# Rounding eight one-hot tables between other copies, and loading them in two pieces, in a recommendation tower

## The reference

```
e = stack([tbl_t[ids[:, t]] for t in range(26)])          # 2048 x 26 x 128
combined = concatenate([dense[:, None, :], e], axis=1)    # 27 features
interactions = einsum('bfd,bgd->bfg', combined, combined)[:, iu, ju]   # upper triangle
h = concatenate([dense, interactions, dense], axis=1)
h = maximum(h @ W_top1 + b_top1, 0)                       # 607 -> 512
h = maximum(h @ W_top2 + b_top2, 0)                       # 512 -> 256
y = h @ W_top3                                            # 256 -> 1
```

## Time and profile before

| | |
|---|---|
| median of three executions | 431.84 us |
| the profiled execution | 434.48 us, of which the span is 432.7 us |
| PE busy | 369.9 us (86%) |
| POOL busy | 276.1 us (64%) |
| DVE busy | 256.5 us (59%) |
| ACT busy | 114.2 us (26%) |
| mean granted clock of TensorE | 0.942 of full |

### The profile page before, as it was taken

The page is one execution under the profiler, slowest core; times in us unless marked ns, Lnnn a source line. Parts: engine busy times, 40 slices in busy tenths (PEclk is TensorE's granted clock), DMA queues, the critical chain, the costliest instruction groups (busy, mean ns, idle before and its releaser), DMA issues.

```text
span 432.7 us, 6765 instructions
## 1 busy us (share of the span) xinstructions
PE 369.9 (86%) x2792; PEld 332.1 (77%) x2792; DVE 256.5 (59%) x368; ACT 114.2 (26%) x235; POOL 276.1 (64%) x295
## 2 busy tenths in 40 slices
PE   0560499996499959999999999999999999999797
PEld 0450499996499948997799979986999799678663
DVE  3254199998088833875389838952588566106410
ACT  2110333322122331322232333322123412321210
POOL 6772277777777777777777777777777777710000
PEclk9996599999599969999999999999899999989999
DMA  5659535444244433444343424343433332310000
GB/s 129 178 165 231 183 84 117 87 79 101 52 93 79 98 56 54 87 100 106 55 91 79 103 52 92 78 100 79 93 77 77 56 53 53 78 21 0 2 0 1
DMA packets 50941, 35.89 MB, mean 83 GB/s; under 512 B 6136, under 2 KB 44664, under 8 KB 50912
## 3 DMA queue, kind: packets, MB, share of 16 engines
q0 software_dynamic: 41472, 18.89, 24.7%
q1 hardware_dynamic: 9440, 16.58, 13.0%
HBM read 35.44 MB, written 0.01 MB: 82 GB/s over the span
## 4 chain that ended last, share of the span: by engine, by line
PE 58%; POOL 18%; issue 7%; DMA 6%; SPq 5%; DVE 3%; ACT 2%; DVEq 0%
POOL E L239 18%; PE psG L347 17%; PE psB L322 16%; PE psB L391 8%; PE psB L398 6%; DMA ET<-tbl 6%; PE psB L386 4%; PE psB L307 3%; SPq L254 2%; PE psB L358 2%; PE psB L405 2%; SPq L251 1%; SPq L247 1%; DVE S L574 1%; PE psB L372 1%
## 5 line engine op out<-in xcount | busy, mean ns | idle before, releaser
L239 POOL DMA_INDIRECT E<-tbl,gidx x288 | 275.4, 956 | 103.9 <-issue 87.0
L552 DVE TENSOR_TENSOR one_hot<-oidx,psR 125x1024 fp32r<-125x1024 int32 x128 | 152.3, 1215 | 39.0 <-PE psB L322 32.2
L322 PE MATMUL psB<-one_hot,tab_hi 125*128 125x256 f32 x512 | 143.2, 311 | 19.5 <-DVE tab_lo L557 13.4
L322 PE MATMUL psB<-one_hot,tab_lo 125*128 125x256 f32 x512 | 133.4, 292 | 0.0
L322 PEld LDWEIGHTS psB<-one_hot,tab_hi 125*128 125x128 f32 x512 | 103.0, 201 | 21.7 <-issue 13.8
L347 PE MATMUL psG<-ET 128*108 128x108 f32 x1024 | 112.5, 265 | 2.0 <-ACT ET L486 1.0
L347 PEld LDWEIGHTS psG<-ET 128*108 128x108 f32 x1024 | 106.6, 180 | 3.1 <-DVE S L574 1.6
L574 DVE COPY_PREDICATED S<-own,psG 108x216 f32<-108x216 int32 x192 | 77.1, 402 | 51.1 <-ACT S L508 44.5
L322 PEld LDWEIGHTS psB<-one_hot,tab_lo 125*128 125x128 f32 x512 | 103.1, 201 | 0.6 <-issue 0.5
L307 PE MATMUL psB<-ident_r,E 128*128 128x128 f32 x288 | 36.7, 253 | 32.0 <-ACT ET L501 18.3
L307 PEld LDWEIGHTS psB<-ident_r,E 128*128 128x128 f32 x288 | 31.0, 145 | 36.4 <-issue 20.0
(11 more groups left out here) (34 smaller groups left out, 149.7 us busy)
## 6 DMA issues: line engine op xcount, KB each, us to landing
oidx<-hot_idx SPq DMA_DIRECT2D x32, 256.0 KB, 3.5
E<-tbl,gidx POOLq DMA_INDIRECT x288
ET<-tbl SPq DMA_DIRECT2D x8, 500.0 KB
dense<-dense_pairs SPq DMA_DIRECT2D x8, 128.0 KB, 3.6
Zd<-dense_rows SPq DMA_DIRECT2D x4, 256.0 KB, 3.1
UH<-W_pairs SPq DMA_DIRECT2D x1, 768.0 KB, 18.6
S<-W_dense SPq DMA_DIRECT2D x1, 512.0 KB, 21.1
w<-W SPq DMA_DIRECT2D x1, 512.0 KB, 13.4
```

The source lines that it names most:

```text
L239: nc.gpsimd.indirect_dma_start(E[:, n % SLOTS, i, :], None, gathered[2 * (n % T_GROUPS) + i // 2].bitcast(f32r), bass.IndirectOffsetOnAxis ...
L322: product = nc.tensor.matmul(bank[:, t % 2 * DUO:(t % 2 + 1) * DUO], tab[0:ROWS_P, t, r, :], one_hot[0:ROWS_P, m % RING, kc, :], start=(r ...
L552: nc.vector.tensor_tensor(one_hot[0:ROWS_P, m % RING], ids, rows, ALU.is_equal).then_inc(hot_full[m % RING], 1)
```

## The change

The change has three parts.

1. ScalarE rounds tables 0 and 1 ahead of the list, and tables 2 to 7 one by one at every second chunk of period 0, where VectorE has its splits already.
2. Each table is loaded by two DMAs, one of 112 partitions (`SPREAD_P`) and one of 13, on the same semaphore; ScalarE waits for 32 instead of 16.
3. SyncE's order: fill 1 and the first dense part come behind table 2, fill 2 behind table 5; the second part of the gather indices and the second dense part come behind table 7.

```
+    SPREAD_P = ROWS_P // 16 * 16
...
             def load_table(h):
-                sp.dma_start(raw_table(h), small[h].rearrange("(p k) d -> p (k d)", k=ROWS_K)
-                             ).then_inc(table_in[h], 16)
+                rows = small[h].rearrange("(p k) d -> p (k d)", k=ROWS_K)
+                for part in (slice(0, SPREAD_P), slice(SPREAD_P, ROWS_P)):
+                    sp.dma_start(raw_table(h)[part], rows[part]).then_inc(table_in[h], 16)
...
             load_oidx(0)
-            load_table(0)
-            load_table(1)
-            sp.dma_start(gidx[:, first:], gather_idx[:, first:]).then_inc(gidx_in[1], 16)
-            for h in range(2, RAW):
+            for h in range(RAW):
                 load_table(h)
-                if h == 3:
+                if h == 2:
                     load_oidx(1)
-                    load_oidx(2)
-            load_dense(0)
-            load_dense(1)
+                    load_dense(0)
+            load_oidx(2)
             for h in range(RAW, NS):
                 sp.wait_ge(lo_ready, h - RAW + 1)
                 load_table(h)
+            sp.dma_start(gidx[:, first:], gather_idx[:, first:]).then_inc(gidx_in[1], 16)
+            load_dense(1)
...
-                act.wait_ge(table_in[h], 16)
+                act.wait_ge(table_in[h], 32)
...
-            for h in range(NS):
+            for h in range(2):
                 round_table(h)
+            rounded_tables = 2
...
-                    elif step[0] == "hot" and step[2] % FILL_CHUNKS == FILL_CHUNKS - 1:
-                        empty_hot(step[1], step[2])
+                    elif step[0] == "hot":
+                        if d == 0 and step[2] % 2 == 0 and rounded_tables < NS:
+                            round_table(rounded_tables)
+                            rounded_tables += 1
+                        if step[2] % FILL_CHUNKS == FILL_CHUNKS - 1:
+                            empty_hot(step[1], step[2])
```

## The result

| | before | changed |
|---|---|---|
| median of 4 executions | 432.36 us (431.76 to 433.13) | 419.44 us (418.33 to 422.52) |
| the profiled execution | 434.48 us, span 432.7 | 420.29 us, span 418.3 |

The ratio is 0.971, 95% interval 0.965 to 0.977: 12.9 us faster in the medians, 14.2 in the profiled executions. Forecast were 417.8 us, 14.0 us faster, and a range of 413.0 to 422.5.

The account below looks back on a forecast made before the run. GpSimd's gather stream was taken as the floor up to turn 71, with a 50.1 us TensorE tail. -14.6 + 0.6 = -14.0 us; 431.84 - 14.0 = 417.8 us, the forecast's own range 414 to 421.5, stated range 413.0 to 422.5.

Parts of the forecast that it names:

- GpSimd's stream is the floor: GpSimd's gathers bound the run up to turn 71; what counts is their earlier end, not TensorE's 18.3 us stall.
- Rival D: TensorE is the bound and its stall and waits all go, 32 us: 399.8 us; chance under 0.01.
- 14.63 us off the stream: GpSimd's 14.93 us stall before gather 24 goes entirely, less the normal 0.30 us.
- +0.6 us for the eighth split: VectorE's eighth table split, formerly inside GpSimd's stall, now has a gather beside it and lengthens it: +0.6 us.
- Faster landing, 2.5 to 3 us a table: Two DMAs per table on SyncE's queue land a table in 2.5 to 3 us instead of 5.49.
- The deadline of 68.0: TensorE's first gram must start by 68.0 us to reach turn 17 when gather 71's data is there; forecast 60.
- Part 1 is what takes the stall away: ScalarE's new rounding order alone removes GpSimd's whole stall; earlier tables are worth nothing directly.
- 9 us in hand: Turn 1, wanted by gather 24 at 36.1 us, is ready 9 us or more earlier even at the old table rate.
- Rival A: Tables land no faster, so TensorE's first gram is late; gain 12.6 to 3.4 us, middle 8: 423.8 us; chance 0.09.
- A gather is used 1.56 us after it ends: TensorE's turn can use a gather's data 1.56 us after the GpSimd instruction ends, read from gather 71 and turn 17.
- Turn 71 directly behind its gather, and the same tail: Turn 71 starts 0.2 us after gather 287's data is usable; TensorE's 50.1 us tail behind it stays unchanged.
- that term: TensorE's clock: half clock from 386.2 to 389.6 us costs 1.7 us in the tail; a drop more or less counts alike.

Follow-up runs that it names:

- the pair with and without PSUM: Changed kernel plus 12 VectorE sums in period 0: both inputs in SBUF, 426.3 us; second input broadcast from PSUM, 420.0 us.
- loads alone: Changed kernel with all eight table roundings ahead of ScalarE's list again, keeping two DMAs a table and SyncE's new order: 420.6 us.
- The run with one DMA: Changed kernel with each table loaded by one DMA of 125 partitions again, its other parts kept: 425.7 us.
- both late kernels: Kernel before with only ScalarE's new rounding order, 427.8 us; and changed kernel with one DMA a table again, 425.7 us.
- part 1 alone: Kernel before with only ScalarE rounding tables 2 to 7 between its copies, one DMA a table and SyncE's old order: 427.8 us.
- the repeat: The changed kernel itself, unaltered, measured again on the chip of the follow-up runs: 419.5 us, ratio 0.968.
- the three-gather kernel: Changed kernel with three gathers a group from group 5 on, 67 of 288 left out: 441.2 and 442.8 us on two slow chips.

## Why the prediction was right, point by point

- *GpSimd's stream is the floor, and counts instead of TensorE's 18.3 us.* Right, and shown: slowed by 6.4 us the kernel took 6.8 more, sped up by 4.4 it took 4.2 less. In the traces of eight of the runs above, all but those on the two chips where the kernel before took over 520 us, turn 71 starts within 0.15 us of the end of gather 287 plus 1.56. The changed kernel's first trace, 1.6 us late, is the exception. Rival D is out.
- *14.63 us off the stream.* Right: gather 24 waits for nothing. Gather 287 at 365.68, forecast 365.9.
- *+0.6 us for the eighth split.* Wrong in sign: seven gathers are long beside the eight splits, for 3.8 us against 4.26. But the second of VectorE's two weight preparations (L571, 1.75 us) met a gather at its start and made it 2.27 us long, so these cost 1.33 us in place of 0.68. Together +0.2. That splits hold gathers up is shown by the pair with and without PSUM.
- *Faster landing, 2.5 to 3 us a table.* Right where nothing else held them: with loads alone the roundings come 2.2 to 4.1 us apart, 2.9 on average, the last at 28.71. The run with one DMA shows that it was the cut in two. That the 112 partitions did it, and not just a second DMA, isn't shown, as no run cuts a table anywhere else.
- *The deadline of 68.0.* Right as a sign, but not the only limit, nor the one that came last: first grams at 57.4, 58.1 and 67.7 cost nothing, 73.7 and 75.9 cost about 8 and 6 us. In both late kernels turn 17 still waits for its gather (1.73 and 1.49 us), which a late TensorE alone would not do. The gather is late itself, at 102.68 and 104.88 instead of 97.03, because GpSimd had stood still for 7.50 and 8.74 us until turns freed its slots. Less its wait, turn 17 would have come 4.8 and 7.0 us behind the changed kernel's, so TensorE missed its deadline too; which of the two limits costs how much alone, no run here tells. Gather 287 comes at 371.24 and 373.50, 5.6 and 7.8 us late, in the order of the first grams. That the times stand in the other order is in part the tails of the two traces, 53.6 us at a granted clock of 0.84 and 47.5 at 0.98.
- *Part 1 is what takes the stall away, and the faster loads are worth nothing directly.* Wrong as an account of which part gives the gain. The long stall goes by either part, the loads alone reach the whole gain (420.6 us), and part 1 alone about half (427.8). Two steps failed. The working gave turn 1 its 9 us in hand and listed turns 2 to 5, wanted at 41 to 57 us, but never set turn 5 against fill 3; and it didn't ask which load the copies wait for that now stand ahead of table 4, the dense part. Alone, part 1 lets GpSimd wait 4.70 us for turn 2 and 2.80 for turn 5. Rival A was the case of one DMA a table, 423.8 forecast and 425.7 measured; it priced only the late first gram, and the 8.74 us before gather 40 are not in it.
- *A gather is used 1.56 us after it ends.* Wrong up to 50 us: gather 7 ends at 12.99 + 1.98 = 14.97 and its turn runs at 26.00 after 5.43 us of waiting. The windows (columns as in the earlier trace rows) of the changed kernel suggest why: the DMA engines are full of the loads.

```profile
5.00:15.00 10.00, 4.27 (x20) 4.30 (x21) 7.90 (x7) 3.13 (x3) 8.15 (x7) 1.00 1.12 271
15.00:25.00 10.00, 5.24 (x34) 4.63 (x33) 8.31 (x8) 3.47 (x5) 7.75 (x7) 0.93 1.18 240
```

  Of the kernel before the same windows are

```profile
5.00:15.00 10.00, 2.99 (x14) 3.02 (x15) 4.71 (x4) 1.29 (x2) 7.86 (x8) 1.00 0.72 196
15.00:25.00 10.00, 4.33 (x19) 3.74 (x19) 3.58 (x3) 1.84 (x2) 7.56 (x9) 1.00 0.60 170
```

  It cost nothing, since slots are wanted back at 37 us and later, and GpSimd itself was not held up.
- *Turn 71 directly behind its gather, and the same tail.* In the changed kernel's first trace turn 71 came at 369.81 where its data could be used at 368.2, 1.6 us late, and the tail was 48.5 us instead of 50.1; the sum is the same, and that the two cancel is luck. In the repeat both are as forecast: gather 287 ends at 365.78, turn 71 starts 1.55 us later, and the tail is 50.0.

```profile
367.33 0.53 PE L307 MATMUL psB<-ident_r,E 128*128 128x128 f32 x4
```

  What moves the tail is the granted clock in it: 50.1 us at 0.94 before, 50.0 at 0.93 in the repeat, 48.5 at 0.98 in the first trace, which had no dip between 370 and 410 us. Four executions between 418.3 and 422.5 us are as wide as that term: its size was right, and which way it falls I can't tell beforehand.

## What to carry to other kernels

Ask which engine's stream is continuous up to the end, and turn every earlier stall into a deadline for the others against it; a stall that ends before its deadline is free, however long it looks. Each buffer that the stream wants back is a deadline of its own, and all of them have to be checked, not only the first and the last. When a step is moved forward, ask of each of its operands where its load stands in the queue. And a small transfer behind large ones in one queue can cost what the large ones save.

## What was not expected

- A gather that starts beside a VectorE instruction with two SBUF inputs ends about 0.81 us behind it, whatever that instruction's length (0.68, 1.22 or 1.75 us), or after its usual 0.94 us if that is later. An instruction that starts inside a running gather doesn't lengthen that one, but it can the next: the split at 16.94 in the changed kernel leaves the gather at 16.52 at 0.94 us and makes the one at 17.77 1.21.
- Beside the faster loads the data of a gather was used up to 11 us after its instruction had ended, instead of 1.56, while the instructions themselves ran on at 0.94 us.
- On two chips the kernel before took over 20% longer, 527.0 and 525.6 us. In the traces from there single matmuls are as short as elsewhere, and between them TensorE stands idle with nothing named. On the first of the two the three-gather kernel took 441.2 us beside 512.9 and 515.0 of the kernels with all gathers. I can't say why.
